# Adapter-and-LoRA kernel: the last output chunk of the last two batches in one VectorE operation, stored by halves of the partitions

## The reference

```python
y = einsum('bij,bkj->bik', x, cond_weight[adapter_ids])        # 8 x 128 x 512
q = y[:, 107:127, :].mean(axis=1)
routing = softmax(q @ router_W.T + router_b)                     # 8 x 8
base = y @ W.T + b
t = einsum('bsd,erd->bser', y, A)
lora = einsum('bser,eor,be->bso', t, B, routing) * 2.0
return x + base + lora
```

## Time and profile before

| | |
|---|---|
| time, median of 3 runs (lowest, highest) | 71.13 us (70.95, 71.92) |
| the profiled execution: time | 71.09 us |
| its span | 69.4 us |
| PE busy | 64.5 us (93%) |
| DVE busy | 36.2 us (52%) |
| granted TensorE clock | full, whole span |
| stores to memory | 10, together 2.10 MB |

### The profile page before, as it was taken

How to read it: one execution, slowest core, us unless ns; L and a number is a source line. 1 busy time by engine, 2 the same in 40 slices (tenths; PEclk the granted TensorE clock), 3 DMA queues, 4 the chain that set the end, 5 groups by cost and what they waited for, 6 DMA issues and landing times.

```text
span 69.4 us, 1034 instructions
## 1 busy us (share of the span) xinstructions
PE 64.5 (93%) x374; PEld 54.3 (78%) x374; DVE 36.2 (52%) x83; ACT 24.1 (35%) x52; POOL 5.3 (8%) x16
## 2 busy tenths in 40 slices
PE   2997988999999999999999999999999999999930
PEld 1333978999999999888888888888788888889920
DVE  1000004035223769999999998591996432047230
ACT  0800002060305888994889903032003450000000
POOL 4000000000000000000060505160000000000000
PEclk9999999999999999999999999999999999999999
DMA  0479899999999999999633050523047500004822
GB/s 0 136 249 371 272 392 387 408 408 418 391 415 409 409 409 411 411 409 413 255 90 76 3 148 0 151 76 76 5 164 265 181 0 9 0 0 156 298 80 76
DMA packets 7494, 15.30 MB, mean 221 GB/s; under 512 B 832, under 2 KB 4032, under 8 KB 7488
## 3 DMA queue, kind: packets, MB, share of 16 engines
q1 hardware_dynamic: 6944, 14.38, 55.2%
q0 software_dynamic: 256, 0.52, 3.0%
q10 hardware_dynamic: 288, 0.33, 1.6%
HBM read 12.08 MB, written 2.10 MB: 204 GB/s over the span
## 4 chain that ended last, share of the span: by engine, by line
PE 81%; DMA 9%; SPq 5%; issue 1%; DVE 1%; DVEq 0%
PE ps_o L512 30%; PE ps_yT L489 11%; DMA wc_raw<-in_wcT_dram 9%; PE ps_t L512 9%; PE ps_o L542 8%; PE ps_y L489 5%; PE ps_y L503 3%; PE ps_y L505 3%; PE ps_y L504 3%; PE ps_yT L503 3%; PE ps_yT L505 3%; PE ps_yT L504 3%; SPq L192 3%; PE ps_y L512 2%; SPq L197 1%
## 5 line engine op out<-in xcount | busy, mean ns | idle before, releaser
L512 PE MATMUL ps_o<-yT_hi,az_hi 128*128 128x512 f32 (+1 forms) x36 | 13.0, 360 | 0.0
L512 PE MATMUL ps_o<-yT_lo,az_hi 128*128 128x512 f32 (+1 forms) x36 | 12.8, 355 | 0.0
L512 PE MATMUL ps_o<-yT_hi,az_lo 128*128 128x512 f32 (+1 forms) x36 | 12.7, 354 | 0.0
L366 DVE TENSOR_TENSOR wc_lo<-wc_raw,wc_hi 128x1024 fp32r<-128x1024 f32 x8 | 9.4, 1218 | 0.0
L292 ACT CAST wc_hi<-wc_raw 128x1024 fp32r<-128x1024 f32 x8 | 8.1, 1045 | 0.6 <-DMA wc_raw<-in_wcT_dram 0.6
L489 PEld LDWEIGHTS ps_y<-xT_raw,wc_raw 128*128 128x128 f32 x64 | 7.3, 192 | 1.1 <-issue 1.1
L424 DVE SCALAR_TENSOR_TENSOR wc_raw<-ps_o,rest_raw,xT_raw 128x512 f32<-128x512 f32 (+1 forms) x8 | 5.4, 714 | 5.0 <-PE ps_o L542 5.0
L489 PE MATMUL ps_y<-xT_raw,wc_raw 128*128 128x128 f32 x64 | 7.5, 276 | 0.4 <-DMA wc_raw<-in_wcT_dram 0.4
L489 PE MATMUL ps_yT<-xT_raw,wc_raw 128*128 128x128 f32 x64 | 7.5, 276 | 0.4 <-DMA wc_raw<-in_wcT_dram 0.4
L489 PEld LDWEIGHTS ps_yT<-xT_raw,wc_raw 128*128 128x128 f32 x64 | 7.3, 192 | 0.6 <-issue 0.6
L179 POOL DMA_DIRECT2D wc_raw<-wc_raw x8 | 4.5, 565 | 40.2 <-DVE wc_raw L385 40.2
(11 more groups left out here) (72 smaller groups left out, 96.7 us busy)
## 6 DMA issues: line engine op xcount, KB each, us to landing
wc_raw<-in_wcT_dram SPq DMA_DIRECT2D x16, 512.0 KB, 12.6
out_dram<-wc_raw SPq DMA_DIRECT2D x7, 256.0 KB, 2.3
rest_raw<-in_rest_dram SPq DMA_DIRECT2D x2, 512.0 KB, 12.4
xT_raw<-in_xT_dram SPq DMA_DIRECT2D x2, 512.0 KB, 14.6
xT_raw<-in_xT_dram SPq DMA_DIRECT2D x3, 256.0 KB, 7.2
wc_raw<-wc_raw SPq DMA_DIRECT2D x8, 64.0 KB, 2.4
wc_raw<-wc_raw POOLq DMA_DIRECT2D x8, 64.0 KB, 2.2
rest_raw<-in_rest_dram SPq DMA_DIRECT2D x1, 278.0 KB, 8.2
```

What stands on the lines that cost most here:

```text
L366: tt(flat(wc_lo[b % 2][:, part_h, :]), flat(wc_raw[:, b, part_h, :]), flat(wc_hi[b % 2][:, part_h, :]).bitcast(F32), ALU.subtract).then_in ...
L512: last = mm(bank, stat[:, n, c, :], yT[mov][:, c].rearrange("p b s -> p (b s)"), start=(start and c == 0 and k == 0), stop=(stop and c == ...
```

## The change

DVE's two operations for the last chunk of batches 6 and 7 become one over 256 columns. Both stores now wait for this operation, and they are cut otherwise: SP stores both batches of partitions 0 to 63 (64 rows of 1 KB), ACT both batches of partitions 64 to 127 (64 rows of 1 KB). One semaphore, `last_half_ready`, takes the place of two; each store still raises its own semaphore in `last_stored`.

```diff
-        last_half_ready = [sem(f"last_half_ready{i}") for i in range(2)]
+        last_half_ready = sem("last_half_ready")
...
         def store_last_half(queue, i):
-            queue.wait_ge(last_half_ready[i], 1)
-            queue.dma_start(out[PAIRS - 1, :, C - 1, i * S:(i + 1) * S], o_sb[:, PAIRS - 1, C - 1, i])\
+
+            rows = slice(i * P // 2, (i + 1) * P // 2)
+            queue.wait_ge(last_half_ready, 1)
+            queue.dma_start(out[PAIRS - 1, rows, C - 1], o_sb[rows, PAIRS - 1, C - 1].rearrange("p b s -> p (b s)"))\
                 .then_inc(last_stored[C + i], 16)
...
             dve.wait_ge(last_pair_done, 1)
-            for i in range(2):
-                stt(out=o_sb[:, PAIRS - 1, C - 1, i], in0=ps_y[:, i * S:(i + 1) * S], scalar=bias[:, C - 1:C],
-                    in1=xT_raw[:, B - 2 + i, C - 1, :], op0=ALU.add, op1=ALU.add).then_inc(last_half_ready[i], 1)
+            stt(out=o_sb[:, PAIRS - 1, C - 1], in0=ps_y[:, 0:N2].rearrange("p (b s) -> p b s", b=2),
+                scalar=bias[:, C - 1:C], in1=xT_raw[:, B - 2:B, C - 1, :], op0=ALU.add, op1=ALU.add)\
+                .then_inc(last_half_ready, 1)
```

## The result

The changed kernel takes 71.72 us (median of 9 runs, 71.48 to 73.25), the kernel before 71.13 us (median of 9, 70.73 to 71.92). The ratio is 1.0083, 95% interval 1.0059 to 1.0107: slower by about 0.6 us, clear of zero, and above the range of 70.8 to 71.55.

A forecast was written before the change was run, and what follows sets the result against it. PE, busy 93% of the span, bounds the kernel; only the 2.8 us tail was at stake. From 71.09 us, DVE -0.13 and landing +0.20 gave +0.07, 71.16, stated as 71.15; range 70.8 to 71.55.

The forecast's parts named there:

- The part ahead of the tail: Everything up to PE's last matmul (66.60 us) stays as it is; only the 2.8 us after it are at stake.
- the DVE part: DVE's last work: one operation over 256 columns takes 0.48 us in place of 0.61, a gain of 0.13 us.
- The issues: Last stores: SP's leaves 0.13 us later, ACT's 0.13 us earlier; each issue still takes 0.34 to 0.35 us with 64 rows.
- The transfers: Last two stores, in flight together, land 1.8 us after issue instead of 1.6, a loss of 0.20 us; ordinary upper bound 1.9.
- Rival 2: Last stores: a store out of half the partitions is slow in itself, landing after 2.4 us; 71.76 us, chance 0.16.
- Rival 1: Last stores: the two don't disturb each other, each lands in 1.6 us; 70.95 us, chance 0.24.
- Rival 3: DVE's last work: the operation over 256 columns takes 0.61 us, so no DVE time is saved; 71.3 us, chance 0.05.

The follow-up runs named there:

- second profile: The changed kernel itself run once more, for a profile without the late start: 71.77 us, span 70.0.
- the experiment with two operations: Changed kernel with the two DVE operations of before, both halves of the partitions stored after the second: 72.04 us, ratio 1.0162 to the kernel before.
- first profile: The changed kernel unaltered, the profiled execution of its nine runs and the slowest of them: 73.25 us, span 71.5.
- the first experiment: Changed kernel with its stores cut by batch again, 128 partitions of 512 B each, both issued after the one operation: 71.43 us, ratio 1.0058 to the kernel before.
- the single store: Changed kernel with one store of 128 partitions of 1 KB from SP and none from ACT: 71.26 us, ratio 1.0061 to the kernel before.

## Why the prediction was wrong

**The part ahead of the tail** and **the DVE part** held. Of the part ahead this is seen in the second profile of the changed kernel (DVE's last work at 66.76, before at 66.62); the first was late from its loads on. DVE's work was as forecast, 0.48 against 0.61 us, a gain of 0.13, shown by the profile after and by the experiment with two operations, whose tail is 0.12 us longer. The end of the span also came 0.5 us after the last landing.

**The issues**: "with 64 rows I take the same" failed. It is 0.55 us, not 0.34. On its own that wouldn't count, since a landing is taken from the issue's start; but it is the sign of the set-up that counts.

**The transfers** are the step that failed. I took 1.8 us from issue to landing and measured 2.3. I had bounded it by 1.9, the 128 KB store, as if only the amount and the size of the pieces mattered. That bound left 0.3 us for two stores at once (1.9 against 1.6), and this is about what they cost: 0.3 with halves of the partitions, 0.4 by batch. What it left out is the half itself: both stores were to have their first data 0.84 us after the issue, and a store of 64 partitions has them after 1.19 to 1.21. The data, forecast as one lump of 0.5 us at 250 GB/s, took 0.73 us (69.90 to 70.63) at 122 to 239. The runs give this sum for the later store:

| | us |
|---|---|
| ACT's store of batch 7 before, issue to landing | 1.6 |
| one store of 64 partitions, nothing beside it | 2.0 |
| of that, before the first data (1.21 - 0.84) | +0.37 |
| the same with another issued at the same moment | 2.3 |
| forecast | 1.8 |

With the gain of 0.13 us on DVE, 0.4 + 0.3 - 0.13 = 0.57 us, against 0.56 us from the two tails, and 0.59 us between the medians.

**Rival 2** had the right place, and its 71.76 us are 0.04 from the measured 71.72, but I gave it 0.16. Its evidence stood in the rows: SP's block moves out of 32 partitions had issues of 543 to 761 ns and landings of 2.4 us. I put the long issue down to the form of these moves and set the row aside. The mechanism I named (less can be drawn from half the partitions) is the smaller part, 0.45 us of data against 0.35; the larger one, 0.37 us, is set-up before any byte moves. And it isn't complete without the two stores hindering each other. That its time came so near is in part luck: the 2.4 us were those of other transfers, and stood in for 2.0 + 0.3.

**Rival 1** (no disturbance) is refuted by the first experiment: even with stores of 128 partitions, issuing both at once takes 2.0 us to the later landing instead of 1.6. **Rival 3** is refuted by the 0.48 us row.

The 0.27 us between the two stores before were worth something as well: of the 0.65 us in which their data moved, the two stores shared only 0.08, and each landed almost as fast as one alone (1.7 and 1.6 us against 1.6).

No version here that writes the whole output beats the kernel before. The best of the variants in the profile is the single store (tail 2.41 us against 2.25; median 71.26 against 71.11 on the same chip, ratio 1.0061 with the interval above); its times and those of the stores by batch (1.0058) don't tell the two apart. What stays open: why 64 rows need the longer set-up and 96 don't, and where two stores issued at the same moment hinder each other. No run here tells either.

## What to carry to other kernels

Time the last stores of a kernel from issue to landing, each alone and all together, and cut them so that all of them keep 128 partitions (here 1.6 us against 2.0 for the same bytes; of fewer, only 96 and 64 were tried, and 96 had the short set-up). Two stores that leave one after the other, each behind its own piece of work, can beat two that leave together after a shorter, merged one: the gain of 0.13 us on the engine was paid back about three times in flight (0.4 us), even with the better cut. If the nearest row to a new form is an odd one, such as an issue of 0.6 us beside issues of 0.34, price the new form by it before explaining it away.

## What the runs showed of the hardware that was not expected

- In the stores traced here the set-up goes by the number of rows (one per partition), and not gradually: 64 rows have an issue of 0.54 to 0.63 us and first data after 1.19 to 1.29 us; 96 and 128 rows 0.34 to 0.37 us and 0.84 to 0.85 us. Size of row and amount made no difference (512 B or 1 KB; 32 and 64 KB with 64 rows, 64 and 128 KB with 128).
- Partitions 0 to 63 give 146 GB/s in a store of 64 KB, partitions 32 to 95 give 196 GB/s (one execution each).
- Of two stores of 64 partitions issued at the same moment from SP and ACT, one starts its data as if alone and the other 0.28 us later (69.90 and 70.18 in the first profile, 68.48 and 68.76 in the second), and it is not always the same queue.
